# Sorting edges by node in a graph layer: broadcast of the places in two halves, from 16 copies in DRAM

## What is computed

```python
q = (x[src] @ qW).reshape(e, HEADS, dh)
k = (x[dst] @ kW).reshape(e, HEADS, dh)
v = (x[dst] @ vW).reshape(e, HEADS, dh)
scores = clip(einsum('ehd,ehd->eh', q, k), -10, 10)
exp_s = exp(scores)
norms = segment_sum(exp_s, src, N)[src]
w = exp_s / (norms + 1e-8)
res = segment_sum(w[:, :, None] * v, src, N).reshape(N, d)
out = layernorm(x + (x + res))
```

## Time and profile before

| | |
|---|---|
| median of three runs | 1666.95 us (1665.98 to 1668.39) |
| the profiled execution | 1672.0 us, its span 1670.2 us |
| busy over the span | PE 1465.2 us (88%), DVE 1431.4 (86%), ACT 1019.1 (61%), POOL 912.8 (55%) |
| DMA | 465.03 MB, mean 278 GB/s |
| q1 (SP), q0 (POOL), q10 (ACT) | 54.2%, 24.1%, 0.2% of 16 engines over the span |
| granted TensorE clock | 0.946 in the mean |

### The profile page before, as it was taken

The page is one execution under the profiler, slowest core; times in us unless marked ns, Lnnn a source line. Parts: engine busy times, 40 slices in busy tenths (PEclk is TensorE's granted clock), DMA queues, the critical chain, the costliest instruction groups (busy, mean ns, idle before and its releaser), DMA issues.

```text
span 1670.2 us, 56304 instructions
## 1 busy us (share of the span) xinstructions
PE 1465.2 (88%) x19964; PEld 1407.4 (84%) x19965; DVE 1431.4 (86%) x2940; ACT 1019.1 (61%) x1836; POOL 912.8 (55%) x768
## 2 busy tenths in 40 slices
PE   5854988898888888888769999999999999999992
PEld 3744878787787878888769999999999999999992
DVE  5889999898988998899258888888888888888897
ACT  4342666566666665666546666666666666666665
POOL 6240777677767777777734444444444444444442
PEclk8566999999999999999979999999999999999996
DMA  7672999999999999899979767677777777777742
GB/s 222 221 274 102 352 367 354 346 331 374 355 328 357 358 357 338 348 364 355 351 286 299 240 241 246 237 248 240 243 247 238 244 245 239 246 242 240 247 157 58
DMA packets 159483, 465.03 MB, mean 278 GB/s; under 512 B 37026, under 2 KB 59298, under 8 KB 152276
## 3 DMA queue, kind: packets, MB, share of 16 engines
q1 hardware_dynamic: 120916, 300.70, 54.2%
q0 software_dynamic: 35840, 163.36, 24.1%
q10 hardware_dynamic: 2688, 0.46, 0.2%
HBM read 271.21 MB, written 209.73 MB: 288 GB/s over the span
## 4 chain that ended last, share of the span: by engine, by line
PE 76%; DVE 10%; issue 7%; DMA 4%; SPq 1%; ACT 1%; DVEq 0%; POOL 0%; POOLq 0%; ACTq 0%
PE two_a L1188 13%; PE meta L1250 13%; PE sum_bank L1250 12%; PE two_b L1188 11%; PE two_a L1271 7%; PE two_b L1271 7%; PE one_d L1261 3%; PE one_c L1261 3%; DMA work<-kv_table 2%; PE meta L1206 2%; PE one_d L1217 2%; DVE work L1523 1%; DVE work L1530 1%; PE sum_bank L1170 1%; DVE cols_work L1368 1%
## 5 line engine op out<-in xcount | busy, mean ns | idle before, releaser
L654 POOL DMA_INDIRECT sorted_rows<-work x448 | 498.9, 1114 | 210.4 <-issue 144.5
L716 POOL TENSOR_TENSOR work<-work 128x768 f32<-128x768 f32 x236 | 352.2, 1492 | 440.7 <-ACT work L979 440.7
L1188 PE MATMUL two_a<-work 128*128 128x192 bf16 x2688 | 265.1, 249 | 88.6 <-issue 86.1
L1188 PEld LDWEIGHTS two_a<-work 128*128 128x128 f16 x2688 | 217.0, 99 | 109.5 <-issue 89.5
L937 ACT ACTIVATE work<-two_a 128x768 f32<-128x768 f32 x224 | 181.5, 810 | 150.0 <-PE two_a L1188 148.2
L1188 PE MATMUL two_b<-work 128*128 128x192 bf16 x2688 | 264.7, 250 | 0.0
L988 ACT ACTIVATE work<-work 128x1024 f32<-128x1024 bf16 x236 | 247.2, 1048 | 0.0
L1250 PE MATMUL sum_bank<-work 128*128 128x100 f32 x1888 | 235.9, 278 | 3.6 <-DVE acc L1601 3.6
L1250 PE MATMUL meta<-work 128*128 128x100 f32 x1888 | 235.9, 278 | 0.9 <-DVE acc L1601 0.9
L1634 DVE TENSOR_REDUCE work<-work 128x32 f32<-128x768 f32 x236 | 225.0, 953 | 8.2
L1188 PEld LDWEIGHTS two_b<-work 128*128 128x128 f16 x2688 | 223.1, 99 | 6.3
(11 more groups left out here) (235 smaller groups left out, 2186.6 us busy)
## 6 DMA issues: line engine op xcount, KB each, us to landing
work<-sorted_rows SPq DMA_DIRECT2D x472, 392.0 KB, 3.5
work<-sorted_local SPq DMA_DIRECT2D x56, 1024.0 KB
sorted_rows<-pad_rows SPq DMA_DIRECT2D x49, 392.0 KB, 4.6
work<-kv_table SPq DMA_DIRECT2D x112, 144.0 KB
sorted_rows<-work POOLq DMA_INDIRECT x448
kv_table<-work SPq DMA_DIRECT2D x12, 576.0 KB, 3.4
work<-in_x SPq DMA_DIRECT2D x12, 192.0 KB, 4.4
out<-acc SPq DMA_DIRECT2D x6, 384.0 KB
```

The lines of the kernel that those rows point to most:

```text
L654: pool.indirect_dma_start(out=rows_dram, out_offset=bass.IndirectOffsetOnAxis(ap=place_now[:, p, u, b:b + 1], axis=0), in_=payload[:, p, u ...
L716: pool.tensor_tensor(now[:, :, 0:D].rearrange("p c (h f) -> p c h f", h=HEADS), blk[:, k, :, :, D:2 * D].rearrange("p m c (h f) -> p (m c) ...
L1188: mm = pe.matmul(to, picked[:, u % 2, k * P:(k + 1) * P], window[:, u, :, n, :], start=(n == 0), stop=(n == 2))
```

## The change

- The DRAM tensor of places gets 16 copies of its 8 KB for each parity, 256 elements (512 B) apart. ACT's one DMA writes them all: its source is 8 partitions of 512 elements, each taken 16 times.
- For that form PE turns the places with four transposes (8 columns each) in place of one, into the PSUM bank `one_c` in place of `meta`, and ACT copies 8 x 512 in place of 32 x 128.
- The broadcast is two DMAs, one for each u, of 512 KB: copy r is read by partitions 8r to 8r + 7, 4 KB each. SP issues them as: window 0, wait for `local_out`, half 0, window 1, half 1. Each has a semaphore of its own (`brow_in[u]`); half u waits for `pick(u)` of two steps earlier, and `pick(u)` for half u alone. ACT waits for both halves of two steps before, ahead of its write.
- The counting semaphores `pool_turn` and `sp_turn` become one, `turn`, with as many increments by POOL. `work` grows by 152 words a partition.

```diff
     CLEAR_STEPS = 10
+    COPIES = 16
+    COPY_GAP = 256
+    TURNS = 4
+    TURNED = QUAD * NCH // TURNS
     CLEARS = 4
...
     kv3 = nc.dram_tensor("kv3_table", (NTAB, 3 * 2 * D), BF16).ap()
     rows_dram = nc.dram_tensor("sorted_rows", (SORTED, RUN * WROW), F32).ap()
-    local_dram = nc.dram_tensor("sorted_local", (2, QUAD * NCH, P), F16).ap()
+    PLACES = QUAD * NCH * P
+    local_dram = nc.dram_tensor("sorted_local", (2, COPIES, PLACES + COPY_GAP), F16).ap()
...
-        WORK = 28360
+        WORK = 28512
...
-        local_v, at = share(at, [P], F16)
-        local_rows, at = share(at, [P], F16)
+        local_v, at = share(at, [QUAD * NCH], F16)
+        local_rows, at = share(at, [TURNS * P], F16)
...
-        turned_v = meta[:, 0:P // 2].bitcast(F16)
+        turned_v = one_c[0:TURNED, 0:TURNS * P // 2].bitcast(F16)
...
-        brow_in = sem("brow_in")
+        brow_in = sems("brow_in", QUAD)
...
-        pool_turn = sem("pool_turn")
-        sp_turn = sem("sp_turn")
+        turn = sem("turn")
...
 
+            def places_of(u, b, half, landed, picks):
+                if not zero(b):
+                    sp.wait_ge(brow_in[u], landed)
+                if not (isinstance(b, int) and b < 2):
+                    sp.wait_ge(pick_made[u % GSEM], picks)
+                    sp.sem_inc(turn, 1)
+                sp.dma_start(brow[:, half, u, :].rearrange("p o w -> p (o w)"),
+                             local_dram[half, :, u * NCH * P:(u + 1) * NCH * P].rearrange("o r w -> (o r) w")
+                             .unsqueeze(1).to_broadcast([COPIES, P // COPIES, NCH * P])).then_inc(brow_in[u], 16)
+
             def emit(a, b, c, p=None):
                 following = c is None or not isinstance(c, int) or c + 1 < NQ
                 if c is None and b == 1:
@@ -810,21 +825,14 @@
                 if c is not None and following:
                     window_of(0, los[0], at_c)
                 if b is not None:
-                    half = bass.ds(low_bits(sp, b, 1), 1)
+                    landed, picks, half = times(sp, b, 16), plus(sp, b, -1), bass.ds(low_bits(sp, b, 1), 1)
                     sp.wait_ge(local_out, times(sp, b, 16, 16))
-                    sp.sem_inc(sp_turn, 1)
-                    if not zero(b):
-                        sp.wait_ge(brow_in, times(sp, b, 16))
-                        sp.sem_inc(sp_turn, 1)
-                    if not (isinstance(b, int) and b < 2):
-                        sp.wait_ge(pick_made[(QUAD - 1) % GSEM], times(sp, b, G2, -G2))
-                        sp.sem_inc(sp_turn, 1)
-                    sp.dma_start(brow[:, half].rearrange("p o u w -> p (o u w)"),
-                                 local_dram[half].rearrange("o r p -> o (r p)").to_broadcast([P, QUAD * NCH * P])
-                                 ).then_inc(brow_in, 16)
-                if c is not None and following:
-                    for u in range(1, QUAD):
-                        window_of(u, los[u], at_c)
+                    sp.sem_inc(turn, 1)
+                for u in range(QUAD):
+                    if b is not None:
+                        places_of(u, b, half, landed, picks)
+                    if c is not None and following and u + 1 < QUAD:
+                        window_of(u + 1, los[u + 1], at_c)
...
-                    act.activation(local_v[:, 0:QUAD * NCH].rearrange("p (u j) -> p u j", u=QUAD), sort_ps[:, :, TW:TW + NCH], ACT.Copy)
+                    act.activation(local_v.rearrange("p (u j) -> p u j", u=QUAD), sort_ps[:, :, TW:TW + NCH], ACT.Copy)
...
                 if b is not None:
                     if not zero(b):
                         act.wait_ge(local_out, times(act, b, 16))
                     act.wait_ge(local_turned, b1)
-                    act.activation(local_rows[0:QUAD * NCH, :], turned_v[0:QUAD * NCH], ACT.Copy).then_inc(local_rows_made, 1)
+                    act.activation(local_rows[0:TURNED], turned_v, ACT.Copy).then_inc(local_rows_made, 1)
                     if not (isinstance(b, int) and b < 2):
-                        act.wait_ge(brow_in, times(act, b, 16, -16))
+                        read = times(act, b, 16, -16)
+                        for u in range(QUAD):
+                            act.wait_ge(brow_in[u], read)
                     act.wait_ge(local_rows_made, b1)
-                    act.dma_start(local_dram[bass.ds(low_bits(act, b, 1), 1)].rearrange("o r p -> (o r) p"),
-                                  local_rows[0:QUAD * NCH, :]).then_inc(local_out, 16)
+                    act.dma_start(local_dram[bass.ds(low_bits(act, b, 1), 1), :, 0:PLACES]
+                                  .rearrange("o r (a w) -> a (o r) w", a=TURNED),
+                                  local_rows[0:TURNED].unsqueeze(1).to_broadcast([TURNED, COPIES, TURNS * P])
+                                  ).then_inc(local_out, 16)
...
                 def turn_places():
                     pe.wait_ge(values_kept, b1)
-                    pe.transpose(turned_v, local_v, ident_h[:]).then_inc(local_turned, 1)
+                    for k in range(TURNS):
+                        mm = pe.transpose(turned_v[:, k * P:(k + 1) * P],
+                                          local_v.rearrange("p (a k) -> p a k", k=TURNS)[:, :, k], ident_h[:])
+                    mm.then_inc(local_turned, 1)
...
                 def pick(u):
-                    if u == 0:
-                        dve.wait_ge(brow_in, times(dve, c, 16, 16))
+                    dve.wait_ge(brow_in[u], times(dve, c, 16, 16))
                     before(kv_made[KPARTS - 1], u)
                     dve.tensor_scalar(picked[:, u % 2], brow[:, half, u, :].rearrange("p o w -> p (o w)"),
                                       node_col[:], None, ALU.is_equal).then_inc(pick_made[u % GSEM], 1)
```

More of the change, by code:

```diff
@@ L108, in gnn_program @@
     assert NG == HG * NBATCH and NBATCH % PB == 0 and NB <= HI * LO and HROWS <= P and TT <= P and NT <= CLEARS * (TI + 1)
-    assert RB == KPARTS and RUN == KPART and FULL + NT <= NBLK and FULL <= 512 and PIECES == 7 and TI == 12 and COLS * P <= 2048
+    assert QUAD == GSEM and RB == KPARTS and RUN == KPART and FULL + NT <= NBLK and FULL <= 512 and PIECES == 7 and TI == 12 and COLS * P <= 2048
     HEAD_SLOT = 1
@@ L648, in scatter @@
                     group_done(pool, tag_kept, u, at_c)
-                pool.sem_inc(pool_turn, 1)
+                pool.sem_inc(turn, 1)
                 for b in range(RB):
```

## The result

The changed kernel takes 1746.12 us (median of five, 1743.6 to 1760.5) against 1668.39 for the kernel before: a ratio of 1.0488, 95% interval 1.0446 to 1.053. It is 78 us slower; the forecast was 30 us faster. The profiled execution took 1754.1 us, its span is 1752.4.

The account below looks back on a forecast made before the run. Bounds: DMA 0.96 full and window 1's loop of landing and use. Step 12.17 to 11.6 us, between POOL's 11.36 and 11.3 / 0.96 = 11.8; 0.57 saved over 53 steps is 30 us: 1637, range 1614 to 1678.

Parts of the forecast that it names:

- The reading side of the copies: Broadcast reads in q1, sorting stage: 16 copies cut 4.38 us a step per engine to 3.40, 0.98 less.
- The writing side: ACT's write of 128 KB in place of 8 KB: 0.65 us a step on 8 engines, less 0.04.
- The DMA sum: DMA load per sorting step: 11.68 - 0.98 + 0.61 = 11.3 us on the fuller engines, 10.7 on the rest.
- The halves: Half the broadcast moves behind window 1 in SP's queue: no DMA time saved, its worth is the order.
- The transposes and ACT's copy: On PE's path in a sorting step: 0.3 us for three more transposes, 0.33 for the longer copy.
- The floors: Least sorting step each engine allows: POOL 11.36 us, DVE 11.2, PE 11.1, DMA 11.3.
- The slower rival: SP's wait for the local write delays window 1: step 12.85 us, 36 us more, 1703; 22 in 100.
- L: Time the local write takes to land, from its issue to SP going on: 5.1 us before, up to 10 feared.
- The rival in which nothing moves: Contention slows the reads: DMA 12.3 us on eight engines, order repays the copies; 1662 to 1675 us; 10 in 100.

Follow-up runs that it names:

- h3_spread_source: The kernel before, with the broadcast reading 128 different stretches of 8 KB in place of one 128 times; 1671.64 us, 1.001.
- k1_write_16_rows: The changed kernel with two transposes in place of four, so the places stand in 16 rows of 512 B, not 8 of 1 KB; 1703.88 us, 1.0212.
- k3_halves_only: The kernel before with the broadcast in two halves around window 1, still one copy in 32 rows and one transpose; 1650.89 us, 0.9895.
- h2_one_copy: The changed kernel with one copy written and read in place of 16; halves, four transposes and wide ACT copy stay; 1653.84 us, 0.9895.
- k2_gate_first_copy: The changed kernel reading only copy 0, its write split into copy 0, for which SP waits, and copies 1 to 15, for which ACT waits; 1735.85 us, 1.0397.
- k4_four_read_one: The changed kernel with four copies written in place of 16 and only copy 0 read; 1660.63 us, 0.9952.
- g3_read_one: The changed kernel with all 16 copies written but every partition reading copy 0; 1731.49 us, 1.0368.

## Why the prediction was wrong

**The reading side of the copies failed** ("they are slow when all engines read the same 8 KB": 0.98 us saved, bounds 0 to 1.03, the upper one about 1.05 when worked out again). It measured 0.08 (4.38 to 4.30), the lower bound. The comparison of two windows in the earlier trace rows had a second difference besides the number of readers of one address: one window lay early in a burst and the other late. The forecast said that only the number of readers differs, and that was not so. h3_spread_source, with no address shared at all, reads as slowly (458 and 456 ns a piece early, 316 and 317 late).

**The writing side was half sized** (8 engines, 25.3 GB/s each, +0.61 us on them). The number of engines was right, as far as the 8 completions of each write and k1_write_16_rows tell. The Trainium skill's rule (page "DMA: Bandwidth & Descriptors", section on why a DMA increments its semaphore by 16), that the slowest dimension sets it, is borne out by 136, 272 and 48 packets a write. The price per piece was not: 81 ns for 1 KB, 12.6 GB/s, near the lower rate of the bounds (10.6) and not the one taken. That is 9.6% of 13.56, 1.30 us, 1.25 more than before. The scatters, too, rose from 59.2% of 12.17 to 55.7% of 13.56, 7.20 to 7.55 us, with nothing changed in them.

**The DMA sum** was 11.68 - 0.98 + 0.61 = 11.3. As measured it is 11.64 - 0.08 + 1.25 + 0.35 = 13.16, against a step of 13.56, 0.97 of it. The way from the load to the step, load over 0.96, was right to 1%; its terms were wrong, and the first was large enough to turn the sign. With a 0 for the reads and the dearer pieces (1.55) the forecast's own bounds gave 13.2 / 0.96 = 13.7; the range stopped at 12.4.

**The halves** were costed at nothing but order. k3_halves_only, in which order, pieces of 4 KB in place of 8 and a semaphore for each half come together, is worth 0.48 us a step, 19 us in all: the fill went from 0.956 to 0.990. The Trainium skill's advice against two transfers in halves (page "DMA: Bandwidth & Descriptors", section "Rules for kernel authors") is on halves of the partitions, and its reason is that both use the same engines. Here each half goes to all 128 partitions, and the trace agrees that little work is saved: q1's 36.0% of 12.17 and 36.1% of 11.69 are 4.38 and 4.22 us.

**The transposes and ACT's copy** were put on PE's path with 0.63 us a step. The copy was sized right (L960 takes 0.59, as forecast), the transposes at twice what they took (0.39 in all in place of 0.23, 0.16 more where 0.3 was forecast). But h2_one_copy, which has both, is 3 us above k3_halves_only, which has neither, and that is within the intervals. PE wasn't the limit there, so its path had room.

**The floors** of POOL and DVE, 11.36 and 11.2, were not reached; the fastest step is 11.69, with the DMA at 0.99.

**The slower rival** saw what the trace shows: L went from 5.2 to 9.4 us in the mean, to 11.5 in the step shown, and SP stood still for it. It was not the cause, since k2_gate_first_copy takes the wait away and keeps both the time and PE's wait for windows. I read it as what full engines look like from SP's queue. **The rival in which nothing moves** had the reading side right, reads that aren't freed by copies; it priced the load at 12.3 in place of 13.15 and let the better order pay for it.

Open are why a burst of reads starts slowly, why the pieces of the write and the scatters grow dearer, how much of k2_gate_first_copy is ACT's longer issue (some 28 us at most, as estimated), and whether the windows' order alone helps the kernel before, since that run fell on a chip with another limit.

## What to carry to other kernels

Where DMA engines are nearly full, as here at 0.96, sum the load of the fullest engine before anything else: a transfer that runs on half of them counts twice there, and the mean share hides it (0.92 was full). The packets of a queue divided by its DMAs, less the data pieces, gave here the number of engines that took part. Before paying for copies of a source, read other addresses once in the same form: that costs one run and says whether the address is the matter.

## What was not expected of the hardware

- Reading 128 different stretches of 8 KB takes as long as reading one 128 times (q1 4.32 and 4.38 us a step). In both, a piece of 8 KB takes some 457 ns within 6 us of the issue and 317 later. Block loads, too, ran at 19.6 GB/s per engine in their first 4 us against 24.7 afterwards.
- A piece of 1 KB from SBUF to DRAM took 47 ns in k4_four_read_one, 67 in g3_read_one and 81 in the changed kernel, though the fullest engines were 0.98, 0.97 and 0.97 busy: the price differed at nearly the same busy share, and no run shows by what.
- One kernel took 1668 to 1671 us on some chips and 1928 and 1944 us on two others, with gaps of 0.4 to 0.5 us between matmuls of one group and the DMA queues at 72%.
